# Three layers of products and matmuls: Strassen's scheme in two more blocks, a new order in layer 1

## What is computed

```python
prev = x0 = inputs                                   # (2048, 39, 16)
for i in range(3):
    Wr = Ws[i].reshape(h, M, 128)                    # h = 39, then 64
    z = relu(einsum('bhk,bmk,hmf->bfk', prev, x0, Wr) + bs[i][None, :, None])
    results.append(z[:, :64])
    prev = z[:, 64:]
pooled = sum(concatenate(results, axis=1), axis=-1)
out = pooled @ W_lin
```

## Time and profile before

| | |
|---|---|
| median of 3 runs | 1955.07 us (1955.04 to 1956.12) |
| the profiled execution | 1955.95 us, of which the span of the profile is 1954.1 us |
| PE busy | 1948.5 us, 100% |
| DVE busy | 1884.1 us, 96% |
| ACT, POOL busy | 649.7 us (33%), 256.3 us (13%) |
| granted clock of PE | 1.00 over the whole span |
| moved by DMA | 326.42 MB, 167 GB/s |

### The profile page before, as it was taken

The page is one execution under the profiler, slowest core; times in us unless marked ns, Lnnn a source line. Parts: engine busy times, 40 slices in busy tenths (PEclk is TensorE's granted clock), DMA queues, the critical chain, the costliest instruction groups (busy, mean ns, idle before and its releaser), DMA issues.

```text
span 1954.1 us, 31455 instructions
## 1 busy us (share of the span) xinstructions
PE 1948.5 (100%) x10864; PEld 786.4 (40%) x10864; DVE 1884.1 (96%) x1329; ACT 649.7 (33%) x760; POOL 256.3 (13%) x298
## 2 busy tenths in 40 slices
PE   9999999999999999999999999999999999999999
PEld 3333444444444444444444344444444434444333
DVE  8989999999999999999999999999999999999988
ACT  2332234432244322344223442224432244422332
POOL 1001101111011111111111111101111111111000
PEclk9999999999999999999999999999999999999999
DMA  7998987788887889878798778987879878789710
GB/s 166 191 195 173 199 173 163 163 176 189 182 173 154 174 174 196 175 151 175 161 202 180 155 167 165 199 189 150 169 166 191 193 156 166 164 178 201 149 40 1
DMA packets 139165, 326.42 MB, mean 167 GB/s; under 512 B 34001, under 2 KB 60010, under 8 KB 139141
## 3 DMA queue, kind: packets, MB, share of 16 engines
q1 hardware_dynamic: 98051, 294.66, 68.4%
q0 software_dynamic: 40320, 31.21, 11.1%
q10 hardware_dynamic: 770, 0.23, 0.1%
HBM read 294.72 MB, written 0.01 MB: 151 GB/s over the span
## 4 chain that ended last, share of the span: by engine, by line
PE 97%; DVE 1%; ACT 0%; DMA 0%; ACTq 0%; issue 0%; DVEq 0%
PE acc L874 32%; PE acc L753 23%; PE acc L953 19%; PE acc L879 17%; PE acc L942 2%; PE acc L745 2%; PE acc L820 1%; PE acc L960 1%; DVE prod L424 1%; PE acc L967 1%; DMA bias<-b 0%; ACT prev L1095 0%; PE acc L760 0%; ACTq L1192 0%; DVE prod L426 0%
## 5 line engine op out<-in xcount | busy, mean ns | idle before, releaser
L424 DVE TENSOR_TENSOR prod<-prev,x_bc 128x2048 f32<-128x2048 f32 x511 | 1142.4, 2286 | 38.1 <-PE acc L960 22.5
L874 PE MATMUL acc<-prod,w_sb 128*64 128x512 f32 x2912 | 659.5, 593 | 0.0
L953 PE MATMUL acc<-prod,w_sb 128*64 128x512 f32 x1064 | 461.3, 592 | 0.0
L960 PE MATMUL acc<-prod,w_sb 128*64 128x512 f32 x728 | 344.4, 592 | 0.0
L874 PEld LDWEIGHTS acc<-prod,w_sb 128*64 128x64 f32 x2912 | 203.8, 137 | 343.5 <-issue 310.4
L1141 ACT ACTIVATE diff<-acc 64x256 f32<-64x256 f32 x56 | 21.3, 380 | 794.2 <-PE acc L879 793.5
L879 PE MATMUL acc<-prod,w_sb 128*64 128x256 f32 x1344 | 282.6, 379 | 0.0
L1057 ACT ACTIVATE prev<-acc,bias 32x1024 f32<-32x1024 f32 x252 | 279.1, 1108 | 3.6
L753 PE MATMUL acc<-x_rot,w_sb 128*64 128x512 f32 x1240 | 277.5, 593 | 0.0
L426 DVE TENSOR_TENSOR prod<-prev,x_bc 128x1024 f32<-128x1024 f32 x193 | 230.0, 1219 | 10.1 <-ACT prev L1041 10.1
L953 PEld LDWEIGHTS acc<-prod,w_sb 128*64 128x64 f32 x1064 | 144.4, 137 | 219.8 <-issue 179.5
(11 more groups left out here) (98 smaller groups left out, 1203.3 us busy)
## 6 DMA issues: line engine op xcount, KB each, us to landing
x_bc<-x SPq DMA_DIRECT2D x312, 256.0 KB, 13.8
x_bc<-x SPq DMA_DIRECT2D x124, 512.0 KB, 20.6
x_rot<-x SPq DMA_DIRECT2D x155, 312.0 KB
x_rot<-x SPq DMA_DIRECT2D x217, 156.0 KB
x_bc<-x SPq DMA_DIRECT2D x124, 128.0 KB, 8.8
x_rep<-x SPq DMA_DIRECT2D x62, 192.0 KB
x_bc<-x_bc POOLq DMA_DIRECT2D x84, 128.0 KB, 3.3
x_t<-x SPq DMA_DIRECT2D x64, 128.0 KB, 9.2
```

The lines of the kernel that those rows point to most:

```text
L424: mul = nc.vector.tensor_tensor(prod[:, s:s + w, :], twice, x_bc[:, u, t:t + w, :], ALU.mult)
L874: mm = nc.tensor.matmul(acc1[f, h, :], w[:, f], prod[:, s, BANK * h:BANK * h + BANK], start=False, stop=stop, skip_group_check=closed)
L953: nc.tensor.matmul(acc2[0:HALF, u, :], w, prod[:, s, 0:BANK], start=(pos == 1), stop=False)
L960: mm = nc.tensor.matmul(acc2[HALF:P, u, :], w, prod[:, s, BANK:NB], start=(pos == 1), stop=False)
```

## The change

Block 1 and block 30 now use the scheme in layers 1 and 2: DVE forms the extra products and the mix there, POOL the sums of tiles for block 1 too, and PE calls the functions for pairs. The second group of six chunks follows the first directly, at position 8 instead of 10; positions 14 and 15 hold what stood at 8 and 9. The mix follows the last product of layer 1, ahead of all products of layer 0. In odd blocks the half chunk is the last of layer 1, not the first (ORDER_ODD): it waits for the mix, closes both sums, and the leftovers of layer 0 come right behind it; then come the second halves of positions 16 to 18. In layer 2 DVE waits for a free slot only from position 10 on. Counts of the semaphores are moved by one block throughout, since block 1 takes part; ACT uses `copy_part` and `evacuate1_by_half` in blocks 1 and 30.

```diff
-    SIX_AT = 2, 10
-    ORDER_PAIRED = [CH - 1, 0, *range(1, 1 + SIX), *range(1 + SIX, T), *range(T + 2, T + 2 + SIX), T, T + 1,
+    SIX_AT = 2, 8
+    ORDER_PAIRED = [CH - 1, 0, *range(1, 1 + SIX), *range(T + 2, T + 2 + SIX), *range(1 + SIX, T), T, T + 1,
                     *range(T + 2 + SIX, CH - 1)]
...
-    BY_HALF = 17
+    ORDER_ODD = [0, T, *range(1, 1 + SIX), *range(T + 2, T + 2 + SIX), *range(1 + SIX, T), *range(T + 2 + SIX, CH - 1),
+                 T + 1, CH - 1]
+    RUNS_ODD = [(0, 1), (1, 1), *((p, 2) for p in range(2, CH - 2, 2)), (CH - 2, 1), (CH - 1, 1)]
+    BY_HALF, BY_HALF_ODD = 17, 16
...
@@ DVE, products2
-                    if pos > 0:
-                        dve.wait_ge(chunk_used, first + (pos + w - (1 if slots is SLOT2 else 0)))
+                    if pos > 0 and slots is not SLOT2:
+                        dve.wait_ge(chunk_used, first + (pos + w))
+                    elif pos > RING2:
+                        dve.wait_ge(chunk_used, first + (pos + w - 1))
@@ DVE, the program
             product_left(1 + U)
-            products1(1, 1, 1, 2 * CH)
+            products1_paired(1, 1, 1, 1, 2 * CH, ORDER_ODD, RUNS_ODD)
+            mix(1, 1)
             products0(2)
...
+            dve.wait_ge(mix_added, 1)
             channel_sum01(0, 0, 1)
...
-                    products1_paired(i, u, j + u, j, i * (2 * CH))
-                    products0(i + 1, range(U - u))
+                    if u == 0:
+                        products1_paired(i, u, j + u, j, i * (2 * CH))
+                    else:
+                        products1_paired(i, u, j + u, j + 1, i * (2 * CH), ORDER_ODD, RUNS_ODD)
                     mix(i, u)
-                    products0(i + 1, range(U - u, C0))
+                    products0(i + 1)
...
-            products1(LAST - 1, 0, STEPS - 1, n)
+            products1_paired(LAST - 1, 0, STEPS - 1, STEPS - 1, n)
+            mix(LAST - 1, 0)
+            dve.wait_ge(mix_added, LAST - 1)
             channel_sum2(LAST - 3, 1)
@@ POOL
-            for n in range(len(PAIR_TILES)):
-                add_tile(0, n, 16 * QPT)
-            with pool.Fori(1, STEPS - 2) as j:
+            for u in (1, 0):
+                for n in range(len(PAIR_TILES)):
+                    add_tile(u, n, 16 * QPT)
+            with pool.Fori(1, STEPS - 1) as j:
@@ PE
+            def split_closing(w, s, u):
+
+                for h in (1, 0):
+                    k = slice(HALF * (h ^ u), HALF * (h ^ u) + HALF)
+                    for o in range(2):
+                        f = slice(HALF * o, HALF * o + HALF)
+                        mm = nc.tensor.matmul(acc1[f, h, :], w[k, f], prod[k, s, 0:BANK], start=False, stop=(h == 0),
+                                              skip_group_check=(h == 1))
+                return mm
...
-            def layer1_paired(i, u, runs, ahead=None):
+            def layer1_even(i, u, runs):
...
-                if ahead is not None:
-                    layer0_left(range(U), ahead)
+
+            def layer1_odd(i, u, runs, ahead):
+                pe.wait_ge(res01_ready, i * 2 + 2)
+                for pos in range(BY_HALF_ODD):
+                    c = ORDER_ODD[pos]
+                    if pos in SIX_AT:
+                        six_chunks(i, u, SIX_AT.index(pos), runs)
+                    elif not any(p < pos < p + SIX for p in SIX_AT):
+                        pe.wait_ge(prod_ready, runs + RUN_OF_ODD[pos] + 1)
+                        one_half(w1_sb[:, c, :], pos % RING, 0, start=(pos == 0))
+                        one_half(w1_sb[:, c, :], pos % RING, 1, start=(pos == 0),
+                                 stop=(pos == BY_HALF_ODD - 1)).then_inc(chunk_used, 1)
+                for pos in range(BY_HALF_ODD, CH - 1):
+                    pe.wait_ge(prod_ready, runs + RUN_OF_ODD[pos] + 1)
+                    one_half(w1_sb[:, ORDER_ODD[pos], :], pos % RING, 0)
+                pe.wait_ge(prod_ready, runs + RUN_OF_ODD[CH - 1] + 1)
+                pe.wait_ge(mix_added, i)
+                pe.sem_inc(left_asked, 1)
+                split_closing(w1_sb[:, ORDER_ODD[CH - 1], :], (CH - 1) % RING, u).then_inc(half_full, 1)
+                layer0_left(range(U), ahead)
+                for pos in range(BY_HALF_ODD, CH - 1):
+                    one_half(w1_sb[:, ORDER_ODD[pos], :], pos % RING, 1,
+                             closed=True).then_inc(chunk_used, 2 if pos == CH - 2 else 1)
...
-            layer1(1, 1, 2 * NR, ahead=PAIR0 + 1)
+            pe.wait_ge(w1_sums_ready, 4)
+            layer1_odd(1, 1, 2 * NR, PAIR0 + 1)
             layer0(0, PAIR0 + 2)
-            layer2(1, 1, 3 * NR)
+            pe.wait_ge(w2_diff_ready, 1)
+            layer2_paired(1, 1, 3 * NR)
...
-            layer1(LAST - 1, 0, n)
+            layer1_even(LAST - 1, 0, n)
...
-            layer2(LAST - 1, 0, n + NR, range(1, TAIL), slots=SLOT2_END)
+            layer2_paired(LAST - 1, 0, n + NR, range(1, TAIL), SLOT2_END)
             layer1(LAST, 1, n + NR + TAIL_RUNS, CH + TAIL, run_of=RUN_OF_LAST)
-            layer2(LAST - 1, 0, n + 2 * NR, range(TAIL, CH), slots=SLOT2_REST)
+            layer2_paired(LAST - 1, 0, n + 2 * NR, range(TAIL, CH), SLOT2_REST)
```

More of the change, by code:

```diff
@@ L63, in cin_kernel @@
     RUN_OF_PAIRED = [n for n, (_, w) in enumerate(RUNS_PAIRED) for _ in range(w)]
-    BY_HALF = 17
+    ORDER_ODD = [0, T, *range(1, 1 + SIX), *range(T + 2, T + 2 + SIX), *range(1 + SIX, T), *range(T + 2 + SIX, CH - 1),
+                 T + 1, CH - 1]
+    RUNS_ODD = [(0, 1), (1, 1), *((p, 2) for p in range(2, CH - 2, 2)), (CH - 2, 1), (CH - 1, 1)]
+    RUN_OF_ODD = [n for n, (_, w) in enumerate(RUNS_ODD) for _ in range(w)]
+    BY_HALF, BY_HALF_ODD = 17, 16
     MIX = 5
@@ L100, in cin_kernel @@
     assert RUN_OF[TAIL] == TAIL_RUNS and all((CH + TAIL + p) % RING + w <= RING for p, w in RUNS_LAST)
-    assert sorted(ORDER_PAIRED) == list(range(CH)) and all(p % RING + SIX <= RING for p in SIX_AT)
+    assert sorted(ORDER_PAIRED) == list(range(CH)) == sorted(ORDER_ODD) and len(RUNS_ODD) == NR
+    assert all(p % RING + SIX <= RING for p in SIX_AT)
     with ExitStack() as ctx:
@@ L493, in more_products, with products1_paired @@
                 nc.vector.tensor_tensor(more, second, twice, ALU.add).then_inc(more_ready, 1)
-            def products1_paired(i, u, loads, added, first):
+            def products1_paired(i, u, loads, added, first, order=ORDER_PAIRED, runs=RUNS_PAIRED):
                 group = {t0: g for g, (t0, _) in enumerate(XB_GROUPS)}
                 group[T1], group[T2] = BC_T1, BC_T2
-                for n, (pos, w) in enumerate(RUNS_PAIRED):
-                    a, t = CHUNKS[ORDER_PAIRED[pos]]
+                for n, (pos, w) in enumerate(runs):
+                    a, t = CHUNKS[order[pos]]
                     if a == 0 and t in group:
@@ L507, in products1_paired @@
                     if pos - RING in SIX_AT:
-                        dve.wait_ge(more_ready, i * 2 + (SIX_AT.index(pos - RING) - 3))
+                        dve.wait_ge(more_ready, i * 2 + (SIX_AT.index(pos - RING) - 1))
                     dve.wait_ge(chunk_used, first + pos + w)
-                    product(1, n, u, order=ORDER_PAIRED, runs=RUNS_PAIRED)
+                    product(1, n, u, order=order, runs=runs)
                     if pos + w - SIX in SIX_AT:
@@ L868, in layer1, with one_half @@
                         by_halves(acc1, w1_sb[:, c, :], prod[:, s, :], False, pos == CH - 1).then_inc(chunk_used, 1)
-            def one_half(w, s, h, stop=False, closed=False):
+            def one_half(w, s, h, start=False, stop=False, closed=False):
                 for o in range(2):
@@ L945, in layer2, with layer2_paired @@
                     mm.then_inc(chunk_used, 2 if pos == 1 else 1)
-            def layer2_paired(i, u, runs):
-                pe.wait_ge(res2_ready, i + 1)
-                for pos in range(1, CH):
+            def layer2_paired(i, u, runs, part=range(1, CH), slots=SLOT2):
+                if part[0] == 1:
+                    pe.wait_ge(res2_ready, i + 1)
+                for pos in part:
                     a, t = CHUNKS[ORDER[pos]]
-                    w, s = w2_sb[:, ORDER[pos], :], SLOT2[pos]
+                    w, s = w2_sb[:, ORDER[pos], :], slots[pos]
                     pe.wait_ge(prod_ready, runs + RUN_OF2[pos] + 1)
@@ L995, in _ @@
                     if u == 0:
-                        layer1_paired(i, u, i * (2 * NR))
+                        layer1_even(i, u, i * (2 * NR))
                         layer0(1, j * (1 + U * C0) + (PAIR0 + 2 + C0 - (1 + U * C0)))
                     else:
-                        layer1_paired(i, u, i * (2 * NR), ahead=j * (1 + U * C0) + (PAIR0 + 1))
+                        layer1_odd(i, u, i * (2 * NR), j * (1 + U * C0) + (PAIR0 + 1))
                         layer0(0, j * (1 + U * C0) + (PAIR0 + 2))
@@ L1200, in _ @@
             act.wait_ge(small_loaded, 16 * SMALL)
-            for i in range(U):
```

(7 more changed lines are left out.)

45 lines of the change are left out of this document (20 added, 25 removed).

## The result

Before 1955.60 us (median of 8 runs, 1955.04 to 1956.31), after 1961.61 us (8 runs, 1959.76 to 1962.00), a ratio of 1.0029, 95% interval 1.0020 to 1.0037. Forecast were 1957.2 us and a range up to 1961.0. The sign of the sum was right and its size too small.

What follows compares the result with a forecast made beforehand. PE was taken to bound the kernel, with DVE close behind. Pairs +1.7, block 1 +1.1 and block 30 -0.7 summed to +2.1 us, giving a median of 1957.2 us, range 1951 to 1961.

Steps and rivals of the forecast that it cites:

- The sign of the sum: Whole kernel: pairs +1.7, block 1 +1.1, block 30 -0.7, together +2.1 us, so slightly slower.
- The even block: Even loop blocks: DVE waits about 2.1 us at the mix's last addition; PE stands 0.27 us at layer 2's position 18.
- The odd block: Odd loop blocks: half chunk last in layer 1 saves one change of matmul rows, 0.15 us each, 2.1 us over 14.
- The pair: One odd and one even block of the loop: net +0.12 us, 14 times +1.7 us; a pair of 120.6 us.
- The slot wait: Layer 2, DVE's wait before position 8: removing it buys nothing on the path.
- Block 30: Block 30 with the scheme: PE 1.2 us earlier, then 0.5 us waiting for DVE in layer 2; net -0.7 us.
- Late by 1 to 3 us, it holds DVE: Block 1: the third tile sum lands 1 to 3 us after DVE wants it at 92.5, and DVE waits.
- I take 2.3: Block 1: stall taken as 2.3 us, less 1.2 saved, so +1.1 us, from -0.4 to +2.6.
- The scheme's 1.22 us: Layer 1 of blocks 1 and 30: Strassen's scheme saves PE 1.22 us per block, 2.4 in all.
- The step's own prices: Block 1: position 18 is 0.8 us late without a late landing, 2.0 with 1 us, some 3.8 with 3 us.
- the third lands at 93.4 to 95.4: Block 1: third tile sum, issued on POOL at 83.4 to 84.7, lands at 93.4 to 95.4 us.
- A sum landing after 97: Rival, block 1 alone costs more: one time, 3 to 5 us more, 1960 to 1962 us; chance 0.07.

Runs made afterwards that it cites:

- the cover: Edit of the kernel after: two of six layer 0 products put ahead of the mix again in even blocks and block 30; pair of blocks 120.33 us.
- 11: Kernel after with the cover, left product and channel sum moved later on DVE in block 1, tiles of block 1 still asked for late; 1956.58 us, 1.0004.
- 9: Kernel after with eight filler matmuls on PE in block 1, ahead of its wait for the third pair's products; 1963.29 us, ratio 1.0036.
- 10: Kernel after with two small DVE operations behind the mix in each even block of the loop; 1968.95 us, ratio 1.0065.
- experiment 2: Kernel after with the cover alone; 1957.65 us, ratio 1.0008 to the kernel before.
- 12: Kernel after with two filler matmuls on PE in block 1, ahead of its wait for the third pair's products; 1961.71 us, ratio 1.0030.

## Why the prediction missed

**Right, with its size.** The even block: DVE's wait ahead of the mix (2.07 us, forecast about 2.1), none in odd blocks, no wait at position 8, PE late at position 18 by 0.28 us (forecast 0.27). The odd block: with the cover, which takes the stall of the even block away, the 14 pairs together are 2.1 us shorter than before, forecast 2.1 for the half chunk. The pair: 120.63, forecast 120.6. The slot wait: nothing. Block 30: -0.70, forecast -0.7. For the pair I multiplied 0.12 by 14 and measured 0.147, since the next step of PE is 0.05 longer too: 0.4 us in all.

**The step that failed: block 1, "Late by 1 to 3 us, it holds DVE", and with it "I take 2.3".** The scheme's 1.22 us were right, the stall was not: 4.4 us in the profiled execution (3.18 + 1.22) and 5.2 by the medians (4.0 + 1.2). The mechanism was right, a late sum that holds DVE and a DVE that then holds PE up to position 18 of layer 2. The term that was mis-sized is DVE's wait: 3.8 us. The step's own prices, 0.8 without a late landing, 2.0 with 1 us and 3.8 with 3, go on to 4.6 at 3.8 us, an estimate, and 4.4 came (4.7 from PE's start on layer 1 of this block). Of the 4.4 us between the forecast of 1957.2 and the measured 1961.61, block 1 has 2.9 by the medians; 0.5 is the median of before (1955.07 on record, 1955.60 now), 0.4 the pairs, and 0.6 is more than the medians can assign.

The step said "the third lands at 93.4 to 95.4", from two transfers of the same kind that had taken 10.0 and 10.7 us. In the six profiles in which this sum is issued late, DVE got it at 95.18, 95.67, 96.92, 96.92, 98.06 and 98.45 (runs 11, after, 9, 10, 2, 12), five of six past my late end; from its issue it took 10.7 to 12.9 us. Block 1 follows one for one, but for the 0.24 us of experiment 2: in after, 10 and 2, whose code in block 1 is the same, the landings of 95.67, 96.92 and 98.06 go with ends of block 1 at 152.37, 153.62 and 155.00. So the usual execution of after probably has a later sum than the profiled one, near 95.67 + 1.15 = 96.8, an estimate, since no other execution of it was profiled. Two rows of one execution gave me a spread of 0.7 us where it is over 3. And DVE wanted the sum at 91.86, not at 92.5.

*The clock, which I had left out, cost next to nothing.* The step priced an idle of PE at its length, and behind 1.95 us of idle PE lost about 1.7 us more at half clock. This term was missing from the forecast and from every rival. Yet block 1 ends 56.7 us behind the landing with the slow clock (after, 10, 12) and without it (11), because DVE was later than PE in either case. The Trainium skill (TensorE: Matmul & The Clock Gate, HAM oscillation) describes idles of PE as what costs the clock. This case's rows agree: 0.50 behind the idle, 1.00 with PE at work in the same place.

**The rival.** "A sum landing after 97" I gave 0.07 and 3 to 5 us. Its time was right, its condition is not shown: the profiled execution, with 1960.46 us already in its span, has the landing at 95.67. Block 1 cost 2.1 us more than forecast there (3.18 less 1.1). The chance was low because I took the spread of two rows for the spread of the thing. An honest late end, the 13.1 us that the tile loads took the earlier trace rows, gives 84.7 + 13.1 = 97.8 and with it a range to 1962.

## What to carry over

When a change moves work to where an engine newly depends on a transfer, price the wait from the slowest landing of any transfer in that traffic, not from the nearest two; and ask for the data earlier before doing anything else: here the order of five lines on SP was worth 4.9 us, four times the arithmetic saved. A slow clock behind a new idle of PE has to be priced on the path and not on PE: here it took 1.7 us of PE's time, and the block ended when DVE let it. Where an engine waits shortly before a stretch in which it has no slack, work moved across the wait costs nothing: two products of layer 0 ahead of the mix gave back 0.3 us in each of 14 pairs.

## What the hardware showed that I had not expected

The clock fell to its lower level after idles of PE of 1.95, 2.69, 3.50 and 3.91 us (after, 12, 10 and 2) in the middle of a program that runs at 1.00 otherwise, and not after one of 1.85 us (11), where eight matmuls took 1.94. In after, 10 and 12 it fell only when PE was at work again, in 2 still during the idle. It was back at 1.00 after 3 to 7 us, and PE had been busy since the idle. The same eight matmuls took 2.69 to 3.68 us in the slow stretch. Clock of the second experiment, behind its 3.91 us:

```profile
97.00:99.00 2.00, 0.00 (x0) 0.00 (x0) 0.94 (x1) 0.00 (x0) 0.00 (x0) 1.00 0.99 223
99.00:101.00 2.00, 0.59 (x2) 0.29 (x4) 1.87 (x2) 0.00 (x0) 0.00 (x0) 0.55 1.09 182
101.00:103.00 2.00, 2.00 (x6) 0.47 (x4) 1.97 (x2) 0.00 (x0) 0.00 (x0) 0.50 1.01 168
103.00:105.00 2.00, 2.00 (x10) 0.95 (x8) 2.00 (x2) 0.00 (x0) 0.00 (x0) 0.50 1.01 238
```

The tile sum of 128 KB, a transfer that adds, took from its issue on POOL at 84.73 to 95.67, 10.9 us, and from 85.51 to 98.45, 12.9 us (after and 12), while DMA was busy all the time; with less traffic some took 2.9. A matmul of 128 columns of weights on 512 in float32, made for filling, took 0.89 us; two of the kernel's own with 64 columns each, which start together, take 0.43.
